# A four-layer graph network on one core: pair-wise node work, a two-chunk TensorE loop, a narrower degree count

## The reference

```
x = LN(x + L0(x))   # relu(x[src] + edge_attr_32), summed over dst, + (1+eps) x
x = LN(x + L1(x))   # softmax attention over dst with cosine scores
x = LN(x + L2(x))   # spline convolution, divided by max(deg, 1); deg = edges per dst
x = LN(x + L3(x))   # five times _pna_layer

def _pna_layer(x, src, dst, edge_attr, eW, eb, pW, pb, poW, pob, lW, lb):
    xt = x.reshape(n, 4, 8)
    ee = edge_attr @ eW + eb
    h = einsum(concat([xt[dst], xt[src], ee]), pW) + pb      # per edge
    ssum, cnt, mx = segment_sum(h, dst), segment_sum(1, dst), segment_max(h, dst)
    mean = ssum / max(cnt, 1);  mx = where(cnt > 0, mx, 0)
    out = einsum(concat([xt, mean, ssum, mx]), poW) + pob
    return relu(out @ lW + lb)
```

## Time and profile before

| | |
|---|---|
| median of 3 runs | 11380.92 us |
| profiled execution, device time | 11385.12 us |
| its span in the trace | 11383.4 us |
| layer 2 on TensorE, first to last L2096 | 2847.0 to 5244.4 us |
| passes of layer 3 (first gather of each) | 5300.6, 6516.6, 7733.2, 8949.7, 10161.8 us |
| busy: PE 92%, DVE 72%, ACT 59%, POOL 71% | granted clock 0.964 in the mean |

### The profile page before, as it was taken

The page is one execution under the profiler, slowest core; times in us unless marked ns, Lnnn a source line. Parts: engine busy times, 40 slices in busy tenths (PEclk is TensorE's granted clock), DMA queues, the critical chain, the costliest instruction groups (busy, mean ns, idle before and its releaser), DMA issues. The chain is left out here.

```text
span 11383.4 us, 153184 instructions
## 1 busy us (share of the span) xinstructions
PE 10496.1 (92%) x55476; PEld 10002.9 (88%) x55476; DVE 8222.9 (72%) x11247; ACT 6684.8 (59%) x6615; POOL 8086.8 (71%) x8215
## 2 busy tenths in 40 slices
PE   4999859996999999998999899989999899989998
PEld 4999848885999999998999899989999899989997
DVE  5776658886888888887666666666666666666666
ACT  2443325554888888885655455554555455545554
POOL 3777777775666666664777677777777677767776
PEclk8999979997999999998999899999999899999998
DMA  7333234434333333332333333333333333333333
GB/s 225 124 115 113 81 66 101 101 100 125 88 89 85 85 89 85 84 88 63 113 110 108 93 108 108 108 108 93 108 109 110 92 110 110 109 93 109 108 108 90
DMA packets 672345, 1170.49 MB, mean 103 GB/s; under 512 B 200361, under 2 KB 458534, under 8 KB 652502
## 3 DMA queue, kind: packets, MB, share of 16 engines
q1 hardware_dynamic: 369098, 833.53, 22.1%
q0 software_dynamic: 287552, 293.65, 12.7%
q10 hardware_dynamic: 15384, 40.39, 1.1%
HBM read 786.62 MB, written 422.62 MB: 106 GB/s over the span
## 5 line engine op out<-in xcount | busy, mean ns | idle before, releaser
L2402 PE MATMUL ps<-qs,oh 128*128 128x416 f32 (+1 forms) x27200 | 5350.1, 352 | 136.9 <-ACT oh L2499 59.7
L2236 POOL DMA_INDIRECT l3g<-TQ,srcs x4440 | 4267.6, 961 | 1527.9 <-issue 1063.9
L2402 PEld LDWEIGHTS ps<-qs,oh 128*128 128x128 f32 x27200 | 4925.0, 188 | 408.8 <-DVE l3g L2587 208.9
L2587 DVE TENSOR_REDUCE l3g<-ps 128x32 f32<-128x416 f32 x3400 | 1918.2, 583 | 1592.0 <-PE ps L2402 1591.5
L2499 ACT CAST oh<-nd 128x1536 fp32r<-128x1536 bf16 x1140 | 1676.1, 1471 | 1727.6 <-DVE nd L2581 1727.6
L2096 PE MATMUL ps<-l2mm,l2oh 128*128 128x408 f32 (+1 forms) x12544 | 2389.9, 352 | 24.4 <-DVE l2mm L2168 24.4
L2096 PEld LDWEIGHTS ps<-l2mm,l2oh 128*128 128x128 f32 x12544 | 2332.7, 188 | 64.4 <-DVE l2mm L2168 25.2
L2080 POOL DMA_INDIRECT l2g<-Y,place x1568 | 1598.3, 1019 | 814.8 <-DVE l2mm L2168 398.7
L2168 DVE TENSOR_TENSOR l2mm<-l2hl,psv 128x1768 fp32r<-128x1768 f32 x784 | 1532.1, 1992 | 261.7 <-PE ps L2096 257.8
L2111 ACT ACTIVATE l2oh<-l2far,l2one 128x512 fp32r<-128x512 f16 x1568 | 1135.2, 724 | 292.6 <-PE ps L2096 290.2
L1211 POOL DMA_INDIRECT l0g<-T,srcs x896 | 968.2, 1081 | 422.5 <-issue 224.8
(11 more groups left out here) (423 smaller groups left out, 7310.3 us busy)
## 6 DMA issues: line engine op xcount, KB each, us to landing
W<-l3o SPq DMA_DIRECT2D x140, 1792.0 KB
mneg<-KG SPq DMA_DIRECT2D x280, 384.0 KB
l3km<-KG SPq DMA_DIRECT2D x280, 360.0 KB
l3g<-TQ,srcs POOLq DMA_INDIRECT x4440
l3t<-AT SPq DMA_DIRECT2D x140, 448.0 KB, 3.9
W<-l1o SPq DMA_DIRECT2D x28, 952.0 KB, 4.0
l0e<-U_a SPq DMA_DIRECT2D x28, 896.0 KB, 4.7
S<-RX SPq DMA_DIRECT2D x49, 512.0 KB
```

Of the source, the lines that this page charges most:

```text
L2236: e.indirect_dma_start(G3[s][:, j, :], None, TQ, bass.IndirectOffsetOnAxis(ap=srcs[:, c * C + j:c * C + j + 1], axis=0)).then_inc(z3[f"g{s ...
L2402: x_ = e.matmul(ps[(KPX * l + k) % 3][:, 0:32 * n], OH[(l + k // SB) % 2][:, g, 128 * (k % SB):128 * (k % SB) + 128], QS[:, p, 32 * n0:32 ...
L2587: e.tensor_reduce(G3[i % 3][:, C - KP + k if k < KP else C - KPE + k - KP, :], ps[r % 3][:, 0:32 * PH].rearrange("p (h f) -> p f h", f=32) ...
```

## The change

1. **Layer 2.** The degree leaves the 34-wide slots. The 14 leading columns of each group's high part are now a one-hot of the node slot, written by a small VectorE operation before each `by_h`; slots are 32 wide. High-part matmuls are 14 + 416 or 14 + 384 = 430 or 398 wide, low-part ones 416 or 384.
2. **TensorE's loop** in a pass of layer 3 holds two chunks and runs 13 times; the last two chunks are written out.
3. **Node work.** `z` only merges `Zb` and `Fx` in place (two operations). `turn_z` takes nodes in pairs (four transposes), `mixed` multiplies pairs with a two-fold matrix `AP` (four matmuls of up to 128 columns). What depends on x and the counts alone is computed with the products of the pass before (`own_rows`, five VectorE operations, out of a second set of products in PSUM bank 7).
4. **SyncE** stores chunk 26 before the last key block of the pass instead of behind it.
5. `set_apart` is one DMA (layers 1 and 3).
6. `weights3` builds the products of matrices that 3 needs: eleven matmuls per pass instead of four.

```diff
-                e.matmul(ps[g][:, 0:F1 * n] ..., MM[...][:, 0:F1 * n] ...)
+                e.matmul(ps[g][:, DG * p:DG + 32 * n], OH2[...], MM[:, q % R2, p, DG * p:DG + 32 * n], ...)
...
             def by_h(u, t):
+                e.tensor_tensor(MM[:, r:r + 2, 0, 0:DG], hpb[:, 2 * n:2 * n + 2, None].to_broadcast([128, 2, DG]),
+                                iot[:, None, 0:DG].to_broadcast([128, 2, DG]), ALU.is_equal)
...
         def set_apart(e, rows, to, signal):
-            for p in range(8):
-                e.dma_start(to[13 * p:13 * p + 13, :], rows[LOW + p:LOW + p + 1, 0:13, :]).then_inc(signal, 16)
+            e.dma_start(to[0:104, :], rows[LOW:128, 0:13, :]).then_inc(signal, 16)
...
                     for m in range(blocks3(i) + 2, blocks3(i + 1) + 2):
+                        if m == blocks3(i) + 2 + NB3 and c:
+                            store(i - 1)
...
-                with nc.Fori(l * NCH, (l + 1) * NCH - 1, ...) as i:
-                    for k in range(KP): pick(l, i, k) ...
+                with nc.Fori(0, NCH // 2 - 1, ...) as t:
+                    for d in range(2):
+                        chunk3(l, t, d, KP)
+                chunk3(l, None, i - 2, KP)
+                chunk3(l, None, i - 1, KPE)
...
+            def products(l, q):
                 if k:
-                    e.wait_ge(*z3.at("qn", k))
+                    e.wait_ge(*z3.at("xa", k))
+                for w_, bank, done in ((WX[0], ps[5], z3["pq"]), (WX[1], ps[7], z3["px"])):
+                    for h, w in ((0, 4), (1, 3)):
+                        i = e.matmul(bank[...], XT[s][0:32 * w, h, :], w_[0:32 * w, 0:64 * w], ...)
+                    i.then_inc(done, 1)
...
+            def own_rows(l, q):
+                e.wait_ge(*z3.at("px", k + 1))
+                XA = pa[:, :, 32:64] + CO ; nd = pb_[:, :, 0:32] * has ; XB = pb_[:, :, 32:64] * cnt
+                nd = nd + XB ; XA = XA + nd          # .then_inc(z3["xa"], 1)
...
+            def z(l, k):
+                Zb[0:32] = Zb[0:32] + Fx[0:32] ; Zb[32:64] = max(Zb[32:64], Fx[32:64])
+            def mixed(l, k):
+                nd = pm[32:64] * rc ; nd = pm[0:32] + nd ; nd = nd + XA ; XC = max(nd, 0)
```

More of the change, by code:

```diff
@@ L69 @@
 R2 = 8
+DG = 14
+MW = DG + 32 * PH
 TURN0 = 2
@@ L2408, in mix @@
-            def mix(l, i, d):
-                if d == 0:
-                    e.wait_ge(*z3.at("e", i * 16 + 16))
-                e.wait_ge(*z3.at("eev", i * 4 + d))
-                for k in range(2 * d, min(2 * d + 2, 7)):
-                    x_ = e.matmul(ps[3][:, 256 * (k % 2):256 * (k % 2) + 256], ET[:, k, :],
-                                  WR[:, l, :, :].rearrange("p a b -> p (a b)"), start=True, stop=True)
-                x_.then_inc(z3["mm"], 1)
+                    e.wait_ge(*z3.at("xa", k))
@@ new lines, in products, with turn_z @@
+                for w_, bank, done in ((WX[0], ps[5], z3["pq"]), (WX[1], ps[7], z3["px"])):
+                    for h, w in ((0, 4), (1, 3)):
+                        e.wait_ge(*z3.at("xts", 2 * k + h + 1))
+                        i = e.matmul(bank[:, 256 * h:256 * h + 64 * w], XT[s][0:32 * w, h, :], w_[0:32 * w, 0:64 * w],
+                                     start=True, stop=True)
+                    i.then_inc(done, 1)
+            def turn_z(l, q):
+                c0, k = GR * ORD[q], NGR * l + q
+                e.wait_ge(*z3.at("z", k + 1))
+                if k:
+                    e.wait_ge(*z3.at("zts", 2 * k))
+                for h in range(4):
+                    n = 64 * min(2, GR - 2 * h)
+                    m = e.transpose(ps[2 * (h // 2)][0:n, (h % 2) * 128:(h % 2) * 128 + 128],
+                                    O3[0][:, c0 + 2 * h:c0 + 2 * h + n // 64, :].rearrange("p c f -> p (c f)"), ident[:, :])
+                    if h % 2:
+                        m.then_inc(z3["zt"], 1)
@@ new lines, in mixed @@
+            def mixed(l, q):
+                s, k = q % 2, NGR * l + q
+                if q == 0:
+                    e.wait_ge(*z3.at("ap", l + 1))
+                if k:
+                    e.wait_ge(*z3.at("masks", k))
+                for h in range(4):
+                    n = 64 * min(2, GR - 2 * h)
+                    e.wait_ge(*z3.at("zts", 2 * k + 1 + h // 2))
+                    m = e.matmul(ps[1][:, 128 * h:128 * h + n], ZT[s][0:n, h, :], AP[0:n, 0:n], start=True, stop=True)
+                m.then_inc(z3["nmm"], 1)
@@ new lines, in chunk3, with at, mix @@
+            def chunk3(l, t, d, n):
+                def at(each, more):
+                    return more + each * d if t is None else t * (2 * each) + (more + each * (l * NCH + d))
+                def mix(s):
+                    if s == 0:
+                        e.wait_ge(*z3.at("wr", l + 1))
+                        e.wait_ge(*z3.at("e", at(16, 16)))
+                    e.wait_ge(*z3.at("eev", at(4, s)))
+                    for k in range(2 * s, min(2 * s + 2, 7)):
+                        x_ = e.matmul(ps[3][:, 256 * (k % 2):256 * (k % 2) + 256], ET[:, k, :],
+                                      WR[:, :, :].rearrange("p a b -> p (a b)"), start=True, stop=True)
+                    x_.then_inc(z3["mm"], 1)
+                for k in range(n):
+                    if k % SB == 0:
+                        e.wait_ge(*z3.at("oh", at(NB3 * PG, PG * (l + k // SB + 1))))
+                    e.wait_ge(*z3.at("red", at(KP, KPX * l + k - 2)))
+                    for g in range(PG):
+                        for p in range(2):
+                            n0, w = PICKS[g]
+                            x_ = e.matmul(ps[(KPX * l + k) % 3][:, 0:32 * w],
+                                          OH[(l + k // SB) % 2][:, g, 128 * (k % SB):128 * (k % SB) + 128],
+                                          QS[:, p, 32 * n0:32 * (n0 + w)],
+                                          start=g == 0 and p == 0, stop=g == PG - 1 and p == 1)
+                    x_.then_inc(z3["pk"], 1)
+                    if k in MIX:
+                        mix(MIX.index(k))
@@ L2683, in layer3_v @@
                 parts(0, g)
+                own_rows(0, g)
             for l in range(5):
@@ L2715, in layer3_v @@
                         parts(l + 1, g - 1)
+                        own_rows(l + 1, g - 1)
                 if l < 4:
@@ L2718, in layer3_v @@
                     parts(l + 1, NGR - 1)
+                    own_rows(l + 1, NGR - 1)
+                    matrices(l + 1)
         block = ctx.enter_context(nc.Block())
```

251 lines of the change are left out of this document (118 added, 133 removed).

## The result

The changed kernel takes **11273.08 us**, median of 4 runs (11270.25 to 11275.03); the kernel before took 11380.81 us (11370.02 to 11386.19) beside it. The ratio is 0.9905, with a 95% interval from 0.9893 to 0.9917. The profiled execution took 11270.25 us, its span is 11268.5 us, 114.9 less than the span before; the forecast's terms come to 97.

A forecast was written before the change was run, and what follows sets the result against it. TensorE's matmuls were taken to bound layer 2 and GpSimd's gathers layer 3's loop; -94 + 11 - 5 + 13 - 12 + 0 - 10 = -97 from 11385 gave 11288, as a median 11284 us, range 11258 to 11333.

The forecast's parts named there:

- Layer 2, -94: Layer 2: 17.5 fewer columns per matmul in the mean, at 0.43 ns each, over 12544 matmuls: -94 us.
- B: Layer 2: VectorE takes over because a small operation costs 0.36 to 0.45 us; at 0.41, 50 us less gain, 11334; 8%.
- C: Layer 2: weight loads set the pace, so -15 us instead of -94, 11363; 4%.
- The loop, 0: Layer 3's passes: 14 fewer loop returns in each save 51 us of TensorE's time, costed at 0 since GpSimd hides it.
- A: Layer 3's loop: GpSimd's 0.3 us gaps follow TensorE's pace, so the loop's saving shows: -51 us more, 11233; 5%.
- E: TensorE's doubled loop: a return costs 5.2 us like a start, +132 us, 11416 in all; 3%.
- (a): Between passes: storing chunk 26 before the last keys shortens the way from last store to first merge of `Fx`: -2.5 us.
- (b): Between passes, from `Fx` to the first relu: two operations instead of six, four transposes and four multiplies: -2.5 us.
- (c): Between passes: a group's period, set by TensorE, goes from 6.30 to 6.1 us: -1 us a transition.
- (d): End of each transition: the seventh group's products wait for `own_rows` of the sixth: +4 us.
- (e): Between passes: SyncE's eight issues no longer hold the last two stores of `QN`: -1.2 us.
- Rival D: Between passes: `own_rows` lengthens every group as before the first pass: +73 us, 11357; 5%.

The follow-up runs named there:

- e7: The changed kernel with 16 columns instead of 14 for the count in layer 2; 11258.43 us.
- e5: The changed kernel with GpSimd leaving out 2 of its 32 gathers in chunks 3 to 26 of every pass; 11163.04 us.
- e11: The changed kernel with the store of chunk 26 back behind the last keys; 11307.57 us.
- e6: The changed kernel with 2 of 32 gathers left out in chunks 3 to 26 and TensorE's old loop of one chunk; 11175.86 us.
- e8: The changed kernel with each pass's last chunk split into 30 picks on TensorE and 26 gathers on GpSimd (32 and 24 before); 11271.43 us.

## Why the prediction was right, point by point

The total came near in part by luck: layer 2 gave 15 us less than its term, and the four transitions 18 more than theirs.

*Layer 2, -94, measured -78.8.* The mechanism, the slope (0.43 ns a column), the price of the small operation (188 ns) and TensorE as the bound are all in the rows. The failed step is "17.5 x 0.43 x 12544", which lets the number of columns alone decide. The mean duration over the eight matmuls went from 351.25 ns (364 and three of 347) to 345.5, which is 5.8, where 17.5 columns are 7.5; with 16 columns (e7) it is 343.9, at 400 columns in the mean, which is 7.35 for 16.5 columns. Rivals B and C are out: VectorE waits 157.9 us for TensorE at L2195 in the 2000 us shown, and the loop is 79 us shorter.

*Weights, +11, measured +6.2.* Right in kind; a turn takes 3.65 us for 4.5. The loads of its first ten matmuls run for 2.4 us (forecast 3.2 for eleven), since those with 64 and 32 columns take 0.05 to 0.1 us each, and four of VectorE's six copies are done or begun before the tenth matmul ends.

*set_apart, -5, measured -2.8.* Inside its bounds, and not told apart from the 3 to 5 us by which unchanged stages move.

*Before the first pass, +13, measured +9.6.* The period was 5.30 for 5.2 at a granted clock of 0.5; at 1.00, which two of the groups had, it was 4.02.

*The loop, 0, measured -2.4.* The result is right and its reason half so. GpSimd is the bound (e5). But "14 x 5 x 0.73 = 51 us of TensorE's time" is wrong: those waits were ScalarE's one-hots, and all 140 are still there. Rivals A and E both rest on a price of the return that is not there. A look at the matmul's row beside the load's would have told.

*Between passes, -12, measured -29.7.* Here the mechanism was wrong, though the measured value lies near the lower bound of -28. Three sums over the four transitions: from the pass's end to the first relu -17.1, for -20 by (a) and (b); from there to the seventh group's `qn` -8.5, where (c) and (d) had +12; from `qn` to the gather -4.1, for -4.8 by (e). So (c) and (d) failed. They kept TensorE at half clock with 6.1 us a group and let `own_rows` stand behind it; in fact the granted clock was back at 1.0 6 to 26 us sooner and VectorE set 4.87. Why it came back sooner isn't settled: TensorE started on the groups only 3 to 4 us sooner. What let the faster groups count is in none of the terms: (a) saw in the early store only the way to `Fx`. Without that store the whole 30 us are gone (e11). The row was there in the kernel before:

```profile
6433.77 0.94 POOL L2220 DMA_INDIRECT l3o<-W,lastq  x1 [9.89 <-SPq L2271]
```

GpSimd idles 9.89 us ahead of its first node row, and behind the last pass, where the store is early already, it has no such wait.

*Behind the last pass, -10, measured -9.5.* The total is right, its parts less so. The first relu came 1.8 us sooner and not 5: from the first merge of `Fx` it is 5.5 us for 7.9, and the merge itself came 0.6 us later. The groups gave the other 7.7, where the forecast had 5.2.

*Rival D* did not happen. The unchanged stages gave 7.5 us that no term had. By the profiled executions the kernel gained 115 us for 97; by the medians it is 108 for 97, because the profiled execution was 4 us above the median before and 3 below it after.

## What to carry to other kernels

An "issue" wait on a weight load is to be read with the matmul's row beside it, and a cost that is put on a loop's return is to be looked for where nothing returns. An early store or load is worth what its slowest reader gains: follow each engine that waits for it, here GpSimd's 49 rows, and not the nearest one. When narrowing an operand, look at where the pieces then begin: with the second matmul's start at byte 64 for byte 56, and half the matmuls two columns wider, the kernel was 15 us faster.

## What the runs showed of the hardware

- In pairs of matmuls (type `F32R` in the kernel) of which the second begins at byte 64 of its rows, 400 and 384 columns took 343 and 337 ns; where it begins at byte 56, 398 and 384 took 345 and 339.
- At a pass's end in the changed kernel the granted clock was at 0.5 for 34 to 38 us in one piece; with 28 and 62 unread matmuls of 512 columns there it was at 0.5 for 7 us in that stretch. It was worth 1.4 us, which these runs can't tell from nothing, since another engine's transfers came next. 88 of them ahead of needed work ran for 21.8 us, and the stage was 12.7 us longer.
- A return of TensorE's loop over a body of some 400 loads and matmuls (e6) or some 800 (e5) did not show: chunks took 39.50 us in the mean with and without one.
- A node row that GpSimd fetches by indirect DMA was there for VectorE 2.4 to 2.6 us behind its issue (runs e8 to e11).
- On one of the chips the same program took 23% longer (13949.81 for 11381 us), with 449 us of TensorE's work in 500 where the other has 500.
